# A 192-byte gap per partition moved from in front of H1_hi to in front of HT_hi

## The chip, the cores and the metric

The kernel runs on one core of a Trainium2 chip. The metric is the device time of one execution in microseconds. Five engines work side by side: TensorE (PE in the profile, with its weight loads shown apart as PEld), VectorE (DVE), ScalarE (ACT), GpSimd (POOL) and the queue of SyncE (SP), which issues nearly all transfers.

## The reference

A graph layer over 50,000 nodes of 256 features and 25,000 edges of 64 features, sorted by target node:

```python
h = jnp.maximum(_layernorm(x, axis=-1), 0.0)
agg = segment_sum(edge_attr_64, dst) / maximum(counts, 1)      # mean of a node's edges, 64 wide
combined = concatenate([agg, h], axis=1)                       # 320 wide
hidden = relu(combined @ W1 + b1)                              # 512 wide
out = x + hidden @ W2 + b2                                     # 256 wide
```

## The kernel before, in words

The nodes are worked through in 98 tiles of 512 (the last has 336), two buffers in turn; tiles 2 to 95 run in a hardware loop with two tiles a pass. Each float32 operand is split into a high part that TensorE's float32r format holds and a low part with the rest, and products are taken as high x high + high x low + low x high.

For one tile: VectorE takes the statistics of the rows X (line 673), GpSimd works out scale and shift (437 to 442), ScalarE writes the normalized rows HN (585), four transfers regroup them into HQ, and VectorE turns them to features x nodes, HT (714). ScalarE rounds HT to HT_hi (597), VectorE subtracts to HT_lo (722). The tile's edges arrive by transfers, are scaled and split on GpSimd and ScalarE (E_both), and TensorE sums them per node with a one-hot matrix OH (lines 901 to 906, seven matmuls of 128 columns). ScalarE and VectorE write these edge sums into QA and QB (602, 604, 726, 728).

Layer 1 on TensorE goes over four blocks m of 128 hidden units. Each block takes six matmuls of 512 columns on the nodes (lines 917, 918 and 919, for two halves c) and two on the edge sums (926 and 927). The weights are the stationary operand, which TensorE loads ahead; HT_hi, HT_lo, QA and QB are the moving operand. The edge sums of the next tile stand behind block 1. ScalarE then rounds the rectified block to H1_hi (611) and VectorE writes H1_lo (732). In layer 2 the roles are the other way round: H1_hi and H1_lo are stationary and the weights w2_both are moving, 512 columns (line 940: high and low weights side by side) and then 256 columns (line 942), 16 such pairs per tile. VectorE adds the result to the rows (743, 746), and SyncE stores them.

The order on each engine is the order of the program text; semaphores hold the engines together. SBUF tiles are placed one behind the other in the order in which `sb(...)` is called, each start rounded up to 32 bytes in the partition. From the sizes this gives, for starts modulo 256 bytes: all weights (w1_hi, w1_lo, wa_hi, wb_lo, w2_both) at 64; X, XB, O, HN and HQ at 192; E_both, OH, HT, HT_hi, HT_lo, QA and QB at 128; then the 192 bytes called `beside`, which nothing reads or writes, and H1_hi and H1_lo at 64.

Of the kernel before, what the change touches and what calls it, by code (L numbers as in the profile page):

```python
# [14 lines left out]
P = 128  # L15
# [11 lines left out]
def build(nc, x, src, dst, edge_attr, w1, b1, w2, b2, out):  # L27
# [41 lines left out]
    with ExitStack() as ctx:  # L69
        def sb(name, shape, dt=F32):  # L70
            return ctx.enter_context(nc.sbuf_tensor(name, shape, dt))
# [65 lines left out]
        E_both = [sb(f"E_both{b}", [P, SUB, 2, DE], F32R) for b in range(2)]  # L137
        OH = [sb(f"OH{b}", [P, SUB, P], F32R) for b in range(2)]
        HT = sb("HT", [P, CD, TILE])
        HT_hi = [sb(f"HT_hi{b}", [P, CD, TILE], F32R) for b in range(2)]  # L140
        HT_lo = [sb(f"HT_lo{b}", [P, CD, TILE], F32R) for b in range(2)]
        QA = sb("QA", [P, TILE], F32R)
        QB = sb("QB", [P, TILE], F32R)
        beside = sb("beside", [P, 48])
        H1_hi = sb("H1_hi", [P, CH, TILE], F32R)
        H1_lo = sb("H1_lo", [P, CH, TILE], F32R)

# [50 lines left out]
        def turned(t, c):  # L198

            return P2[c][:] if isinstance(t, int) and t < 2 else HT[:, c, :]  # L200

# [73 lines left out]
        def moved(t, b):  # L275

            if isinstance(t, int):
                return MOVED * (t // 2)
            return MOVED // 2 * t - MOVED // 2 * b
# [387 lines left out]
        def _(dve):  # L667
# [42 lines left out]
            def transpose(t, b, c):  # L710
                if c == 0:
                    past(dve, s_hlo, 2 * t)
                    dve.wait_ge(s_hq[b], moved(t, b))
                dve.transpose(HT[:, c, :].rearrange("p (j n k) -> p k j n", j=SUB, k=QN),  # L714
                              HQ[b][:, :, c * QP:(c + 1) * QP].rearrange("p (k j) f -> p k j f", k=QN)).then_inc(s_th, 1)
# [316 lines left out]
```

## Time and profile before

| | |
|---|---|
| median of 3 runs | 1337.56 us (1337.38 to 1338.96) |
| profiled execution, its own time | 1337.26 us |
| its span, first to last instruction | 1335.7 us |
| mean granted clock of TensorE | 0.997 of full speed |
| busy: PE, PEld, DVE, ACT, POOL | 1319.7, 1118.0, 1216.5, 697.4, 541.7 us |

Busy is the time an engine has an instruction in it; TensorE's matmuls overlap (one starts while the one before still drains), so its busy time says that it never stands still, not that it is at its peak. The distance between the starts of successive matmuls is the better measure of its speed. The profile's line numbers are those of the listing above.

### The profile page before, as it was taken

What the parts mean: (1) busy time and instruction counts of PE and PEld (TensorE: products, weight loads), DVE (VectorE), ACT (ScalarE), POOL (GpSimd) and SP (SyncE); (2) the same over time, 40 slices, a digit from 0 to 9 for tenths busy, and PEclk for the clock granted to TensorE, in tenths of its full rate; (3) what the DMA queues carried; (4) which work ended last, traced back from release to release, by engine and by line L of the source; (5) the groups of instructions that cost most, each with busy time, mean ns of one, the idle gap of its engine ahead of it and who ended that gap; (6) DMA issues with size and microseconds to landing.
All of it is one profiled execution on the core that took longest, in us unless ns stands there. A gap on an engine that the chain in (4) does not pass through costs nothing.

```text
span 1335.7 us, 29289 instructions
## 1 busy us (share of the span) xinstructions
PE 1319.7 (99%) x6998; PEld 1118.0 (84%) x6998; DVE 1216.5 (91%) x3153; ACT 697.4 (52%) x1285; POOL 541.7 (41%) x707
## 2 busy tenths in 40 slices
PE   6999999999999999999999999999999999999998
PEld 4788888888888888888888888888888888888887
DVE  6899999999999999999999999999999999999997
ACT  5455555555555555555555555555555555555553
POOL 6443434343434343434343434343434343434341
PEclk8999999999999999999999999999999999999999
DMA  4676767676767676767676767676767676767663
GB/s 119 126 126 130 126 130 126 130 126 130 125 131 125 131 125 131 125 131 125 131 125 131 124 132 124 132 124 132 124 132 124 132 123 132 123 133 123 133 111 76
DMA packets 420693, 168.21 MB, mean 126 GB/s; under 512 B 319092, under 2 KB 420230, under 8 KB 420680
## 3 DMA queue, kind: packets, MB, share of 16 engines
q1 hardware_dynamic: 419688, 166.89, 67.2%
q10 hardware_dynamic: 992, 1.18, 0.3%
q14 instruction: 9, 0.07, 0.0%
q8 instruction: 4, 0.07, 0.0%
HBM read 66.25 MB, written 51.40 MB: 88 GB/s over the span
## 4 chain that ended last, share of the span: by engine, by line
PE 93%; SPq 3%; DVE 1%; DMA 1%; issue 1%; POOL 0%; ACT 0%; DVEq 0%; POOLq 0%
PE P L940 25%; PE P L942 13%; PE P L917 13%; PE P L919 13%; PE P L918 13%; PE P L926 6%; PE P L927 6%; PE PA L906 1%; PE PA L905 1%; SPq L324 1%; DMA HQ<-HN 1%; SPq L323 1%; SPq L311 1%; SPq L284 0%; PE PA L901 0%
## 5 line engine op out<-in xcount | busy, mean ns | idle before, releaser
L940 PE MATMUL P<-w_both,H_hi 128*128 128x512 f32 x1564 | 548.4, 392 | 2.5 <-DVE H_lo L732 2.4
L611 ACT ACTIVATE H_hi<-P 128x512 fp32r<-128x512 f32 x392 | 233.9, 598 | 490.7 <-PE P L927 490.7
L942 PE MATMUL P<-w_both,H_lo 128*128 128x256 f32 x1564 | 437.8, 280 | 0.0
L940 PEld LDWEIGHTS P<-w_both,H_hi 128*128 128x128 f32 x1564 | 292.5, 187 | 69.5 <-DVE H_lo L732 3.9
L732 DVE SCALAR_TENSOR_TENSOR H_lo<-P,H_hi 128x512 fp32r<-128x512 f32 x392 | 266.0, 679 | 67.7 <-ACT H_hi L611 64.4
L917 PE MATMUL P<-HT_hi,w_hi 128*128 128x512 f32 x776 | 309.0, 398 | 0.0
L918 PE MATMUL P<-HT_lo,w_hi 128*128 128x512 f32 x776 | 303.3, 391 | 0.0
L919 PE MATMUL P<-HT_hi,w_lo 128*128 128x512 f32 x776 | 303.2, 391 | 0.0
L460 POOL TENSOR_TENSOR XB<-X,b_row 128x1024 f32<-128x1024 f32 x97 | 233.9, 2411 | 167.4 <-DVE O L746 166.1
L942 PEld LDWEIGHTS P<-w_both,H_lo 128*128 128x128 f32 x1564 | 295.2, 189 | 3.6
L454 POOL TENSOR_TENSOR E_both<-ES,E_both 128x256 fp32r<-128x256 f32 x98 | 72.5, 740 | 391.7 <-ACT E_both L591 391.7
L714 DVE STREAM_TRANSPOSE HT<-HQ 128x512 f32<-128x512 f32 x192 | 205.2, 1069 | 1.9 <-DMA HQ<-HN 1.8
L585 ACT ACTIVATE HN<-X,shift,rstd 128x256 f32<-128x256 f32 x388 | 200.3, 587 | 4.0 <-POOL shift L442 4.0
L597 ACT ACTIVATE HT_hi<-HT 128x512 fp32r<-128x512 f32 x192 | 121.6, 633 | 118.9 <-DVE HT L714 118.8
L746 DVE TENSOR_TENSOR O<-P,XB 128x256 f32<-128x256 f32 x391 | 166.0, 425 | 13.3
L919 PEld LDWEIGHTS P<-HT_hi,w_lo 128*128 128x128 f32 x776 | 145.7, 188 | 32.5
L917 PEld LDWEIGHTS P<-HT_hi,w_hi 128*128 128x128 f32 x776 | 145.6, 188 | 28.3
L743 DVE TENSOR_TENSOR XB<-P,XB 128x256 f32<-128x256 f32 x391 | 163.4, 418 | 4.6 <-PE P L942 1.5
L918 PEld LDWEIGHTS P<-HT_lo,w_hi 128*128 128x128 f32 x776 | 146.2, 188 | 23.7
L926 PE MATMUL P<-QA,wa_hi 128*128 128x512 f32 x392 | 153.6, 392 | 0.1
L927 PE MATMUL P<-QB,wb_lo 128*128 128x512 f32 x392 | 152.7, 390 | 0.0
L722 DVE TENSOR_TENSOR HT_lo<-HT,HT_hi 128x512 fp32r<-128x512 f32 x192 | 139.0, 725 | 9.1 <-ACT HT_hi L597 0.8
(87 smaller groups left out, 1196.0 us busy)
## 6 DMA issues: line engine op xcount, KB each, us to landing
out_dram<-O SPq DMA_DIRECT2D x97, 512.0 KB, 4.5
HQ<-HN SPq DMA_DIRECT2D x384, 128.0 KB, 4.1
X<-in_x_dram SPq DMA_DIRECT2D x95, 512.0 KB, 4.3
ER<-in_edge_attr_dram SPq DMA_DIRECT2D x392, 32.0 KB, 1.8
DT<-table_dram SPq DMA_DIRECT2D x392, 1.0 KB, 1.7
X<-in_x_dram ACTq DMA_DIRECT2D x1, 512.0 KB, 5.2
w_raw<-in_L_gnn_W_dram ACTq DMA_DIRECT2D x4, 128.0 KB, 5.1
w_raw<-in_L_gnn_W_dram SPq DMA_DIRECT2D x2, 256.0 KB, 4.3
```

The costliest lines, as they stand in the source:

```text
L460: pool.tensor_tensor(XB[b][:], rows_of(t, b), b2_row[:].unsqueeze(1).to_broadcast([P, SUB, D]), ALU.add).then_inc(s_xb, 1)
L585: act.activation(into, rows, ACT.Relu, bias=shift[b][:, j:j + 1], scale=rstd[b][:, j:j + 1]).then_inc(s_ln, 1)
L611: act.activation(H1_hi[:, m, nodes(t)], bank(m)[:, nodes(t)], ACT.Relu).then_inc(s_1hi, 1)
L714: dve.transpose(HT[:, c, :].rearrange("p (j n k) -> p k j n", j=SUB, k=QN), HQ[b][:, :, c * QP:(c + 1) * QP].rearrange("p (k j) f -> p k j ...
L732: dve.scalar_tensor_tensor(out=H1_lo[:, m, nodes(t)], in0=bank(m)[:, nodes(t)], scalar=0.0, in1=H1_hi[:, m, nodes(t)], op0=ALU.max, op1=AL ...
L917: pe.matmul(bank(m)[:, nodes(t)], w1_hi[:, c, cols], HT_hi[b][:, c, nodes(t)], start=(c == 0), stop=False)
L918: pe.matmul(bank(m)[:, nodes(t)], w1_hi[:, c, cols], HT_lo[b][:, c, nodes(t)], start=False, stop=False)
L919: pe.matmul(bank(m)[:, nodes(t)], w1_lo[:, c, cols], HT_hi[b][:, c, nodes(t)], start=False, stop=False)
L926: pe.matmul(bank(m)[:, nodes(t)], wa_hi[:, cols], QA[:, nodes(t)], start=False, stop=False)
L927: pe.matmul(bank(m)[:, nodes(t)], wb_lo[:, cols], QB[:, nodes(t)], start=False, stop=True).then_inc(s_l1, 1)
L940: pe.matmul(out_bank(j)[some, :], H1_hi[:, m, rows], w2_both[:, m, :, :].rearrange("p a d -> p (a d)"), start=(m == 0), stop=False)
L942: last = pe.matmul(out_bank(j)[some, 0:D], H1_lo[:, m, rows], w2_both[:, m, 0, :], start=False, stop=(m == CH - 1))
```

## The change

The allocation of `beside` moves up by four lines of the program. HT_hi, HT_lo, QA and QB then start 192 bytes later, at 64 modulo 256; HT and all before it, and H1_hi and all behind it, keep their addresses. No instruction is added, removed or moved.

```diff
         HT = sb("HT", [P, CD, TILE])
+        beside = sb("beside", [P, 48])
         HT_hi = [sb(f"HT_hi{b}", [P, CD, TILE], F32R) for b in range(2)]
         HT_lo = [sb(f"HT_lo{b}", [P, CD, TILE], F32R) for b in range(2)]
         QA = sb("QA", [P, TILE], F32R)
         QB = sb("QB", [P, TILE], F32R)
-        beside = sb("beside", [P, 48])
         H1_hi = sb("H1_hi", [P, CH, TILE], F32R)
         H1_lo = sb("H1_lo", [P, CH, TILE], F32R)
```

## Rows read from the trace of the kernel before

**Rows 1.** The page: span, busy time of each engine, granted clock in slices, chain by engine.
```profile
span 1335.7 us, 29289 instructions
PE 1319.7 (99%) x6998; PEld 1118.0 (84%) x6998; DVE 1216.5 (91%) x3153; ACT 697.4 (52%) x1285; POOL 541.7 (41%) x707
...
PEclk8999999999999999999999999999999999999999
...
PE 93%; SPq 3%; DVE 1%; DMA 1%; issue 1%; POOL 0%; ACT 0%; DVEq 0%; POOLq 0%
```
**Rows 2.** Groups by line, matmuls: xcount | busy us, mean ns | idle before.
```profile
L940 PE MATMUL P<-w_both,H_hi 128*128 128x512 f32 x1564 | 548.4, 392 | 2.5 <-DVE H_lo L732 2.4
L942 PE MATMUL P<-w_both,H_lo 128*128 128x256 f32 x1564 | 437.8, 280 | 0.0
L917 PE MATMUL P<-HT_hi,w_hi 128*128 128x512 f32 x776 | 309.0, 398 | 0.0
L918 PE MATMUL P<-HT_lo,w_hi 128*128 128x512 f32 x776 | 303.3, 391 | 0.0
L919 PE MATMUL P<-HT_hi,w_lo 128*128 128x512 f32 x776 | 303.2, 391 | 0.0
...
L926 PE MATMUL P<-QA,wa_hi 128*128 128x512 f32 x392 | 153.6, 392 | 0.1
L927 PE MATMUL P<-QB,wb_lo 128*128 128x512 f32 x392 | 152.7, 390 | 0.0
```
**Rows 3.** Busy time per engine in one tile's stretch, with the granted clock.
```profile
core 0: us, PE busy (x) PEld busy (x) DVE busy (x) ACT busy (x) POOL busy (x), PEclk, DMA share, GB/s
661.00:674.36 13.36, 13.36 (x73) 11.37 (x72) 12.35 (x32) 7.06 (x14) 5.39 (x7) 1.00 0.69 128
```
**Rows 4.** Timeline of PE, steady tiles: start us, duration us, what.
```profile
661.18 0.39 PE L918 MATMUL P<-HT_lo,w_hi 128*128 128x512 f32 x1
...
661.63 0.39 PE L926 MATMUL P<-QA,wa_hi 128*128 128x512 f32 x1
...
667.64 0.40 PE L917 MATMUL P<-HT_hi,w_hi 128*128 128x512 f32 x1
...
671.32 0.22 PE L901 MATMUL PA<-OH,E_both 128*128 128x128 f32 x1
...
671.74 0.44 PE L917 MATMUL P<-HT_hi,w_hi 128*128 128x512 f32 x1
672.02 0.39 PE L918 MATMUL P<-HT_lo,w_hi 128*128 128x512 f32 x1
...
675.45 0.39 PE L940 MATMUL P<-w_both,H_hi 128*128 128x512 f32 x1
...
677.53 0.39 PE L940 MATMUL P<-w_both,H_hi 128*128 128x512 f32 x1
...
681.00 0.40 PE L917 MATMUL P<-HT_hi,w_hi 128*128 128x512 f32 x1
...
682.39 0.39 PE L926 MATMUL P<-QA,wa_hi 128*128 128x512 f32 x1
```
**Rows 5.** Timeline of PE, layer 2 of tile 95, behind a wait.
```profile
1306.18 0.50 PE L940 MATMUL P<-w_both,H_hi 128*128 128x512 f32 x1 [0.56 <-DVE H_lo L732]
...
1306.63 0.40 PE L940 MATMUL P<-w_both,H_hi 128*128 128x512 f32 x1
...
1309.82 0.39 PE L917 MATMUL P<-HT_hi,w_hi 128*128 128x512 f32 x1
```
**Rows 6.** Timeline of DVE: last instructions ahead of their readers on PE.
```profile
676.40 0.67 DVE L732 SCALAR_TENSOR_TENSOR H_lo<-P,H_hi 128x512 fp32r<-128x512 f32 x1
...
681.77 0.29 DVE L728 TENSOR_TENSOR QA<-PA,QA 64x128 fp32r<-64x128 f32 x1
```

## The prediction

> **What bounds the kernel now.** I read the page's busy line and its chain of waits first. TensorE (PE) is busy for 99% of the span and holds 93% of the chain that ended last, while VectorE has 91% and ScalarE 52% of the span [rows 1]. The chain changes hands only in the short stretches at the two ends. The groups by line then say what TensorE does: 3,112 matmuls of layer 1, which is 776 on each of lines 917, 918 and 919 and 392 on each of lines 926 and 927, and 2 x 1564 of layer 2 [rows 2]. The reader should not add up their mean durations (about 390 ns each): the matmuls overlap. What counts is the distance from one start to the next, and that is read in the order of time [rows 4]. One tile of 512 nodes takes 681.00 - 667.64 = 13.36 us, and in such a stretch TensorE is covered for 13.36 us of 13.36 with the clock granted in full, VectorE for 12.35 us [rows 3, 4]. So 98 tiles at 13.36 us are 1309 us of the 1335.7, and nothing outside TensorE's own stream moves the end in the steady part.
>
> The steady tile falls into parts, by starts [rows 4]. Layer 1 from 667.64 to 671.32 is 16 matmuls in 3.68 us, the seven edge sums to 671.74 take 0.42 us (60 ns each), the first matmul after them 0.28 us, the next 15 to 675.45 take 3.43 us (228.7 ns each), and layer 2 to 681.00 is 16 pairs (512 and 256 columns) in 5.55 us, which is 346.9 ns a pair. 512 columns at 2.4 GHz are 213.3 ns, so each step of layer 1 carries some 15 ns that are not columns. Only these 15 ns can answer to an address.
>
> **The change, part by part.** It adds and removes no instruction, wait or transfer. The 192 bytes leave the place in front of H1_hi and stand in front of HT_hi. HT_hi, HT_lo, QA and QB move up by 192 bytes, from 128 to 64 modulo 256. H1_hi and everything behind it stay at their addresses, and so do all tiles up to HT. Three things can feel it.
>
> (a) The 3,112 matmuls of layer 1 (and 24 in the prologue) stream their moving operand from another start, while the weights they are paired with stay at 64. This is on the path. The trace of before has no matmul of layer 1 with both operands at 64, so I bound it by neighbours. The floor is the 213.3 ns of the columns: a gain of at most 228.7 - 213.3 = 15.4 ns x 3,112 = 48 us. For the other side there is the most expensive stream in the trace: behind a wait, layer 2 runs from 1306.63 to 1309.82 in 9 pairs, 354.4 ns a pair, against 346.9 [rows 5]. That is 7.5 ns more a pair at the very same addresses, or 3.8 ns a matmul. On 3,112 matmuls of layer 1 it would be a loss of 12 us, and on layer 2's 1564 pairs likewise 12 us; both ends together are -48 and +24 us. The nearest rows for the value itself are layer 2's, because there both operands already start at 64. A straight line through its pairs and the edge sums (60 ns for 128 columns, both operands at 128, so equal start again) is pitch = a + b x columns with a + 128 b = 60 and 2a + 768 b = 346.9. It gives b = 0.443 ns and a = 3.3 ns, and 230.2 ns for 512 columns. Layer 1 shows 228.7 ns with the starts 64 bytes apart. So the rows allow a loss of 1.5 ns per matmul if equal starts are what costs it. The times in the rows are rounded to 10 ns: the edge sums' 0.42 us over 7 steps leave 1.4 ns either way on each, and with it this difference may be zero. I take zero. The two placements that the trace does show agree within what it can resolve, and a tile of one placement has no reason in these rows to be cheaper.
>
> (b) The writers and readers of the moved tiles on ScalarE and VectorE: lines 597, 602 and 604 (ScalarE), 722, 726 and 728 (VectorE). None of them is on the path. The narrowest cover is the edge sums': VectorE's line 728 ends at 681.77 + 0.29 = 682.06 and TensorE wants QA at 682.39, 0.33 us later. The next is layer 2's: H_lo ends at 676.40 + 0.67 = 677.07 and its first reader in that tile, the seventh pair, starts at 677.53, 0.46 us later [rows 4, 6]. Their time would have to grow by over 0.3 us a tile before TensorE waits; four VectorE instructions stand in that sum (two of line 722, one each of 726 and 728), so each would have to take some 80 ns longer. If it came to that, each further 0.1 us a tile is 9.8 us. I cost it at nothing.
>
> (c) DMA: the row tiles X, HN, HQ and O, the edge windows and the output don't move. No transfer writes or reads a moved tile. Nothing.
>
> The sum is 0 us on the profiled execution's own 1337.26 us (span 1335.7 and 1.6 us around it), which is 0.3 us under the median of 1337.56. I forecast 1337.5 us.
>
> Against an effect of (a) speaks the Trainium skill, SBUF — State Buffer, section "Who interferes with whom": TensorE has two independent read ports, one for the moving operand and one for weight loads, and waits for nobody. By that rule the distance between the two starts cannot matter and the sum stays 0. What the rows add: at one and the same set of addresses a pair costs 346.9 or 354.4 ns [rows 4, 5], so something other than the address sets part of the step; that is consistent with the rule but doesn't prove it.
>
> **The rivals.** *Equal starts cost a little.* Mechanism and place: layer 1 falls onto the line of layer 2 and the edge sums, 230.2 in place of 228.7 ns. Price: 1.5 ns x 3,112 = 4.7 us, or 1342 us; it decides as soon as the step exceeds 229.6 ns (0.9 ns is 2.7 us). For it: two streams with equal starts lie on one line and layer 1 lies under it. Against: the rounding above, and no view names the cause. *Layer 1 hands over in another rhythm, and layer 2 falls into its dear one.* The rows show that layer 2 keeps 354.4 ns a pair from the wait to the end of its stage, so the rhythm holds once entered. The steady tile has 346.9 now. Entered in every tile it costs 7.5 ns x 1564 = 11.7 us: 1349 us. This case and the one before are the other side of the forecast.
>
> *Layer 1 gets cheaper.* Its steps aren't even now: from 661.18 to 661.63 are two steps of 225 ns, where the mean is 228.7 [rows 4]. If the new placement lets all of them run so, it is 3.7 ns x 3,112 = 11.5 us: 1326 us. For it: the short steps exist, and the columns alone would allow more. Against: layer 2, already with equal starts at 64, has no shorter steps than layer 1. *The extra goes altogether.* The step could fall to the columns' own 213.3 ns and a few more; at half of the 15.4 ns the gain is 24 us, 1314 us. Of it the Trainium skill says, TensorE: Matmul & The Clock Gate, section "Back-to-back issue gap", that the warm distance is N / 2.4 + 2.5 ns, 215.8 ns for 512 columns; by that the kernel's layer 1 has 12.9 ns to give, 40 us on 3,112 matmuls, as an estimate from that page. The trace doesn't agree with the figure in any 512-column step, with weights and rows at 64 or at 128, so I give it little. *The change doesn't do what it says:* the order of the tiles sets their addresses, and 128 + 192 is 64 modulo 256; this ends at no change too, and I leave it 2%.
>
> **How the numbers follow.** About 0.2%, 2.7 us, is what a measurement of this kernel can tell from no change. No change 42% (with the 2%), equal starts cost a little 18%, the dear rhythm in layer 2 or in layer 1 14%, shorter steps 22% (from a third of the 11.5 us up), the extra goes altogether 4%. That makes faster 0.26, same 0.42, slower 0.32. The range reaches from 1327 to 1347 us: it holds no change, the 4.7 us and most sizes of both partial cases, and leaves out the full dear rhythm, the full 11.5 us of gain and the large gain. Inside "no change" alone it would be 1336 to 1340 us.
>
> **What the changed profile would show.** If I am right: 13.36 us from one tile's first layer 1 start to the next, 3.43 us for the 15 steps behind the edge sums, 5.55 us for the 16 pairs, no wait before line 926 or 940 in steady tiles, and counts as before. The first rival shows 3.45 us and 13.41 us a tile, with layer 2 as it is. The second shows 5.67 us for the 16 pairs. The third shows under 3.40 us. Line 722's or 726's mean longer by more than 80 ns, with TensorE waiting at line 926, would say that the cover of (b) was the weak step. I am wrong if the tile differs from 13.36 us by more than 0.028 us.

## The result and the profile after

The changed kernel takes 1342.59 us (median of 7 runs, 1341.61 to 1343.77) against 1337.56 for the kernel before (7 runs): ratio 1.0036, 95% interval 1.0026 to 1.0045. The profiled execution took 1342.59 us with a span of 1341.0, against 1337.26 and 1335.7. It is slower by some 5 us, where no change was forecast.

The page's busy time, chain and clock of the changed kernel answer to [rows 1] and say what they said there: TensorE is the bound, with a mean granted clock of 0.998 of full speed and the same instructions.

```profile
span 1341.0 us, 29289 instructions
PE 1324.8 (99%) x6998; PEld 1118.4 (83%) x6998; DVE 1217.3 (91%) x3153; ACT 697.0 (52%) x1285; POOL 541.4 (40%) x707
...
PEclk9999999999999999999999999999999999999999
...
PE 93%; SPq 3%; DVE 1%; DMA 1%; issue 1%; POOL 0%; ACT 0%; DVEq 0%; POOLq 0%
```

Where in the run the time went is read from two starts of the same matmul far apart, the first matmul of tile 4 and the first of tile 95. In the timeline of the kernel before:

```profile
79.80 0.40 PE L917 MATMUL P<-HT_hi,w_hi 128*128 128x512 f32 x1
...
1295.56 0.40 PE L917 MATMUL P<-HT_hi,w_hi 128*128 128x512 f32 x1
```

and of the changed one:

```profile
80.45 0.40 PE L917 MATMUL P<-HT_hi,w_hi 128*128 128x512 f32 x1
...
1301.06 0.40 PE L917 MATMUL P<-HT_hi,w_hi 128*128 128x512 f32 x1
```

Over these 91 tiles it is 1220.61 - 1215.76 = 4.85 us, 53 ns a tile; 0.65 us was lost ahead of them and 0.2 us won back behind. So it is a loss of the steady tile. The groups by line of the changed kernel, the answer to [rows 2], point at layer 2 but not at its size, since mean durations of overlapping matmuls say little:

```profile
L940 PE MATMUL P<-w_both,H_hi 128*128 128x512 f32 x1564 | 557.1, 398 | 3.1 <-DVE H_lo L732 2.9
L942 PE MATMUL P<-w_both,H_lo 128*128 128x256 f32 x1564 | 438.9, 281 | 0.0
L917 PE MATMUL P<-HT_hi,w_hi 128*128 128x512 f32 x776 | 308.5, 398 | 0.0
L918 PE MATMUL P<-HT_lo,w_hi 128*128 128x512 f32 x776 | 303.6, 391 | 0.0
...
L926 PE MATMUL P<-QA,wa_hi 128*128 128x512 f32 x392 | 152.5, 389 | 0.1
```

The timeline of the changed kernel's TensorE shows it; it answers to [rows 4], start first:

```profile
670.64 0.40 PE L917 MATMUL P<-HT_hi,w_hi 128*128 128x512 f32 x1
...
674.29 0.22 PE L901 MATMUL PA<-OH,E_both 128*128 128x128 f32 x1
...
674.70 0.45 PE L917 MATMUL P<-HT_hi,w_hi 128*128 128x512 f32 x1
674.99 0.40 PE L918 MATMUL P<-HT_lo,w_hi 128*128 128x512 f32 x1
...
678.41 0.39 PE L940 MATMUL P<-w_both,H_hi 128*128 128x512 f32 x1
...
678.75 0.40 PE L940 MATMUL P<-w_both,H_hi 128*128 128x512 f32 x1
...
683.70 0.40 PE L940 MATMUL P<-w_both,H_hi 128*128 128x512 f32 x1
...
684.05 0.40 PE L917 MATMUL P<-HT_hi,w_hi 128*128 128x512 f32 x1
```

Layer 1's first half is 3.65 us (before 3.68), its 15 steps from 674.99 are 3.42 us (3.43), and layer 2 is 5.64 us (5.55). From the starts in whole nanoseconds, in nearly every steady tile, layer 1 with the edge sums went from 7.809 to 7.773 us and layer 2 from 5.551 to 5.640. Layer 1, whose operand was moved, became 36 ns cheaper. Layer 2, none of whose addresses changed, became 89 ns dearer: 14 pairs in 683.70 - 678.75 = 4.95 us are 353.6 ns each, close to the 354.4 ns that [rows 5] gave behind a wait. 89 - 36 is the 53 ns.

### The profile page after: what moved, and what is told of

Read it like the earlier page. It is cut to its first block, busy times and chain, and to the rows that moved or that the text cites. A ratio compares the mean times of both kernels' runs of the same rounds, so it can differ in the third digit from the quotient of the medians.

```text
span 1341.0 us, 29289 instructions
## 1 busy us (share of the span) xinstructions
PE 1324.8 (99%) x6998; PEld 1118.4 (83%) x6998; DVE 1217.3 (91%) x3153; ACT 697.0 (52%) x1285; POOL 541.4 (40%) x707
## 4 chain that ended last, share of the span: by engine, by line
PE 93%; SPq 3%; DVE 1%; DMA 1%; issue 1%; POOL 0%; ACT 0%; DVEq 0%; POOLq 0%
PE P L940 26%; PE P L942 13%; PE P L917 13%; PE P L918 13%; PE P L919 13%; PE P L926 6%; PE P L927 6%; PE PA L906 1%; PE PA L905 1%; SPq L323 1%; DMA HQ<-HN 1%; SPq L324 1%; SPq L311 1%; SPq L284 0%; PE PA L901 0%
## 5 line engine op out<-in xcount | busy, mean ns | idle before, releaser
L940 PE MATMUL P<-w_both,H_hi 128*128 128x512 f32 x1564 | 557.1, 398 | 3.1 <-DVE H_lo L732 2.9
L714 DVE STREAM_TRANSPOSE HT<-HQ 128x512 f32<-128x512 f32 x192 | 210.3, 1095 | 1.7 <-DMA HQ<-HN 1.6
L722 DVE TENSOR_TENSOR HT_lo<-HT,HT_hi 128x512 fp32r<-128x512 f32 x192 | 136.0, 709 | 12.1 <-ACT HT_hi L597 7.7
```

Source lines behind the costliest of these rows:

```text
L940: pe.matmul(out_bank(j)[some, :], H1_hi[:, m, rows], w2_both[:, m, :, :].rearrange("p a d -> p (a d)"), start=(m == 0), stop=False)
```

## The experiments

Theory A: the step depends on how weight loads and row stream of TensorE run against each other, through the starts modulo 256 of both and through the timing with which a stage is entered. Theory B: another engine's traffic on the moved tiles disturbs TensorE. "Rows" are the moving operand and "weights" the stationary one; "difference" below is the start of the rows minus the start of the weights, modulo 256. A stream is "settled" when its steps repeat in a fixed pattern.

**Streams by themselves.** A new kernel; its core:

```python
for so in range(0, 64, 16):            # start of the weights, in floats
    for mo in range(0, 64, 16):        # start of the rows
        same(so, mo, 512, 24)          # 24 matmuls of 512 columns
        mark()                         # one small matmul as a mark
# then pairs(so, mo, 12) in the same way; pairs(16, 16, 12) behind mark(64), mark(96), ...
```

> A kernel of its own that leaves the whole computation out: one TensorE runs matmul streams over constant data while all other engines stand still. 24 steps of 512 columns for each pair of starts (weights, rows) at 0, 64, 128 and 192 modulo 256; then 12 pairs of 512 and 256 columns for each of the 16; then such pairs at 64/64 behind one shorter matmul of 64 to 336 columns; then streams of 128, 256 and 384 columns, and one in bf16. Theory A (timing between weight loads and rows inside TensorE, set by both starts): steps at 64 (weights) and 128 (rows) take 228.7 ns as layer 1 did before, steps at 64/64 take 226.7 ns as after, and pairs at 64/64 take 346.9 or 352.5 ns depending on the matmul that they follow. Theory B (the other engines' reads and writes of SBUF slow TensorE down): all 16 placements agree, near 216 ns a step and 325 ns a pair. If starts matter by themselves and not by history, the pairs behind the shorter matmuls all take the same time.

It took 261.17 us. Its timeline on TensorE, for weights at 64 and rows at 0, 64, 128 and 192 in this order (line 67 is the mark):

```profile
38.59 5.83 PE L56 MATMUL A<-R,W 128*128 128x512 f32 x24
44.26 0.19 PE L67 MATMUL A<-R,W 128*64 128x64 f32 x1
44.29 5.71 PE L56 MATMUL A<-R,W 128*128 128x512 f32 x24
49.84 0.19 PE L67 MATMUL A<-R,W 128*64 128x64 f32 x1
49.87 5.76 PE L56 MATMUL A<-R,W 128*128 128x512 f32 x24
55.47 0.19 PE L67 MATMUL A<-R,W 128*64 128x64 f32 x1
55.49 5.82 PE L56 MATMUL A<-R,W 128*128 128x512 f32 x24
61.15 0.19 PE L67 MATMUL A<-R,W 128*64 128x64 f32 x1
```

From the first start to the mark it is 5.67, 5.55, 5.60 and 5.66 us. All 16 placements fall into four groups by the difference alone: 0 gives 5.55 to 5.57 us, 64 gives 5.59 to 5.60, 128 gives 5.65 to 5.66, 192 gives 5.67 to 5.68. Settled, that is 226.7, 228.8, 232.7 and 233.3 ns a step (means over the last 12 steps, from starts in whole nanoseconds). Layer 1 stood at difference 64 before and at 0 after. Settled streams at starts 64 and 64 with fewer columns took 120.0 ns (256 columns) and 173.3 ns (384), by the starts in whole nanoseconds. A bf16 stream comes last in this kernel:

```profile
252.08 5.35 PE L73 MATMUL A<-RB,WB 128*128 128x512 bf16 x24
257.08 0.38 PE L67 MATMUL A<-R,W 128*64 128x64 f32 x1
```

From the first of its 24 starts to the last it is 4.974 us, 216 ns a step. That is the figure which the Trainium skill gives for the warm gap of an isolated matmul (TensorE: Matmul & The Clock Gate, section "Back-to-back issue gap"). The same section has some 131 ns a matmul of 512 columns for a sustained stream with weight loads; no run here shows that, and the streams measured here lie at the isolated figure (bf16) or some 11 to 17 ns above it (float32r).

The pairs at 64/64, behind six matmuls of 512 columns and a mark of 64 columns, and behind the same with a mark of 96:

```profile
177.60 0.39 PE L61 MATMUL A<-R,W 128*128 128x512 f32 x1
...
181.07 0.39 PE L61 MATMUL A<-R,W 128*128 128x512 f32 x1
...
183.36 0.39 PE L61 MATMUL A<-R,W 128*128 128x512 f32 x1
...
186.89 0.40 PE L61 MATMUL A<-R,W 128*128 128x512 f32 x1
```

Ten pairs take 3.47 us in one (first two lines) and 3.53 us in the other, at the same addresses in the same kernel, and each keeps its pace to the end. Marks of 64, 128, 160, 192 and 256 columns led to some 347 ns a pair, 96, 224 and 336 to some 353. So with equal starts there are two rhythms, and the entry picks. The cheap one, 346.7 ns, is the sum of two settled steps, 226.7 and 120.0 ns; the dear one, 353.3, has some 6.6 ns more in every pair. Theory B falls for the stream's pace: nothing else ran here.

**The model tile.** TensorE alone runs the steady tile's matmuls:

```python
tiles(ht=32, qa=32, qb=32)   # starts in floats: the kernel before
tiles()                      # all at 16 floats = 64 bytes: the changed kernel
tiles(ht=32)                 # edge sums only
tiles(qa=32, qb=32)          # rows only
```

> A kernel of its own that leaves the computation out: TensorE alone runs the matmuls of the steady tile in the kernel's order (two layers, edge sums), three tiles per variant, over constant data, with nothing to wait for. Theory A (everything is inside TensorE and follows from the starts and the order): the first four variants, with the starts of the kernel before, of the changed kernel, of edge sums only and of rows only, take 13.36, 13.41, 13.41 and 13.49 us a tile. If another engine's traffic has a part in it, they differ from these. Further variants look for a cheaper tile with rows, edge sums, layer 1 results and weights all at 64: layer 2's long and short matmuls grouped or in alternating order, edge sums behind another block, QB alone or H1_lo alone at 0, 128 or 192, and H1_hi, H1_lo and w2_both together at 0, 128 or 192. By theory A layer 1 keeps 7.77 us in most and layer 2 takes either 5.55 or 5.64 us. Last come steps of 512 columns with 128, 64 and 32 columns of weights: if the extra over 216 ns comes from weight loads that read beside the rows, it shrinks with their width; if it is a property of the row stream, it stays.

It took 895.26 us. The last tile of each of the first two variants, from its first matmul (line 68) to the mark (line 53):

```profile
45.01 0.40 PE L68 MATMUL A<-HT_hi,w_hi 128*128 128x512 f32 x1
...
58.38 0.19 PE L53 MATMUL A<-w_hi 128*64 128x64 f32 x1
...
85.32 0.40 PE L68 MATMUL A<-HT_hi,w_hi 128*128 128x512 f32 x1
...
98.73 0.19 PE L53 MATMUL A<-w_hi 128*64 128x64 f32 x1
```

In nanoseconds the four tiles are 13,361, 13,413, 13,415 and 13,486; the kernels' own are 13,360, 13,413, 13,413 and 13,487. The 53 ns come back to a nanosecond or two with every other engine idle. The model's tiles lie at other places of SBUF than the kernel's and agree with them modulo 256, so that is enough. The same kernel varied the width of the weights: with 128 columns the 24 steps took 5.55, 5.60, 5.66 and 5.67 us at the four differences, with 64 or 32 columns 5.53 to 5.57 us at all of them. The spread between the starts shrinks from 0.13 to 0.04 us and no longer follows the difference; the extra over bf16 stays. The first fits a collision with weight loads, which no run shows by itself; the second says that most of the extra doesn't come with their width.

**Parts of the change, other starts.** The edits are gaps only (48 floats are 192 bytes):

```diff
 e2   gap [P, 48] before QA; none elsewhere              (QA, QB 64; HT_hi, HT_lo 128)
 e3   gap [P, 48] before HT_hi, [P, 16] before QA, [P, 48] before H1_hi   (the reverse)
 e6   gap [P, 32] before HT_hi, [P, 16] before H1_hi     (rows and edge sums 0)
 e7   no gap                                             (H1_hi, H1_lo 128)
 e8   the changed kernel, and [P, 48] before H1_lo       (H1_lo 0)
```

> Only QA and QB begin at 64; HT_hi and HT_lo stay at 128, H1_hi at 64. Theory A: layer 2's rhythm is set by how layer 1 hands over, and the last two matmuls ahead of it read QA and QB. If these two alone set it, layer 2 takes 5.64 us a tile and layer 1 stays near its 7.81 us: 1345 to 1346 us. If the rhythm of the whole layer 1 sets it, layer 2 keeps 5.55 us, some 1337 us. Theory B (the addresses that ScalarE and VectorE write beside layer 2): as HT_hi and HT_lo are three quarters of what they write there, at most a quarter of the 5 us: 1338 to 1339 us.

> HT_hi and HT_lo begin at 64, QA and QB at 128, H1_hi at 64. Theory A with the last two matmuls as the deciding ones: layer 2 keeps 5.55 us and layer 1 takes between 7.77 and 7.81 us, 1334 to 1337.5 us. With the whole of layer 1 as the deciding one: layer 2 5.64 us, 1342 to 1344 us. Theory B: three quarters of the loss, 1341 to 1342 us.

> HT_hi, HT_lo, QA and QB begin at 0 modulo 256, H1_hi and the weights at 64 as before. Theory A by the stream measurements (rows minus weights of 192: 233.2 ns a step against 228.9 at 64 and 226.6 at 0): layer 1 takes 32 x 4.3 = 0.14 us a tile more than in the kernel before, 7.94 to 7.96 us, which is 1351 us, or 1360 us if layer 2 also falls into its dear rhythm. Theory B (the address alone that the other engines write, with no relation to the weights): no reason for a longer layer 1, 1337 to 1343 us.

> No gap at all: HT_hi to QB stay at 128 as in the kernel before, H1_hi and H1_lo begin at 128 too, so layer 2 has rows (w2_both at 64) minus weights of 192. Theory A by the stream measurements: 353.3 ns a pair in place of 346.9, 16 x 6.4 = 0.10 us a tile, 1347 to 1348 us, with layer 1's stage unchanged. If layer 2's rhythm depends only on how layer 1 hands over, nothing changes: 1337.5 us.

> The changed kernel, with a second gap of 192 bytes in front of H1_lo, which then begins at 0 modulo 256; HT_hi, HT_lo, QA, QB, H1_hi and the weights at 64. The model tile of this placement took 13.340 us (layer 1 7.79, layer 2 5.55) against 13.413 for the changed kernel's. Theory A: the kernel's steady tile does the same to some ns, 1337.3 - 96 x 0.020 = 1335.4 us, so the loss is undone without touching what the change moved. Theory B: H1_lo's start has nothing to do with the tiles that the change moved, 1342.6 us stays.

The parts are distances between starts in whole nanoseconds, of the commonest tile of each kernel, in us. Each ratio is taken against runs of the kernel before made beside it, whose medians were 1337.56 us for the changed kernel, e2 and e3, 1337.04 for e6 and e7, and 1337.62 for e8:

| kernel | layer 1 | layer 2 | tile | median us | ratio, 95% interval |
|---|---|---|---|---|---|
| before | 7.809 | 5.551 | 13.360 | 1337.56 | |
| changed | 7.773 | 5.640 | 13.413 | 1342.59 | 1.0036 (1.0026 to 1.0045) |
| e2 edge sums only | 7.857 | 5.556 | 13.413 | 1341.78 | 1.0035 (1.0023 to 1.0046) |
| e3 rows only | 7.845 | 5.642 | 13.487 | 1348.59 | 1.0090 (1.0072 to 1.0108) |
| e6 rows, edge sums at 0 | 7.915 | 5.558 | 13.473 | 1348.80 | 1.0087 (1.0069 to 1.0105) |
| e7 no gap | 7.798 | 5.648 | 13.446 | 1345.15 | 1.0059 (1.0041 to 1.0077) |
| e8 H1_lo at 0 | 7.757 | 5.596 | 13.353 | 1336.97 | 0.9996 (0.9986 to 1.0005) |

e2 is a miss of both forms of theory A as I had written them: the edge sums alone cost the same 53 ns a tile, but in layer 1, not in layer 2. There rows and edge sums differ in start, so each block switches the difference twice, and the steps around a switch are long (231 to 237 ns in place of 225 to 232). e3 pays both and is a miss too: 1348.59 us, where the dearest case that I had written was 1344. Layer 2 is dear in e3 and cheap in e2, so it follows the rows' start and not that of the last two matmuls ahead of it. The model tile, run after these two, gives both, so it is theory A without a shortcut. e6 and e7 are doses: difference 192 costs 0.106 us in layer 1 (0.14 forecast; not every step is a settled one, which would explain the rest) and 0.097 us in layer 2 (0.10 forecast). Both kernels came out 2 to 3 us under their forecasts of 1351 and 1347 to 1348 us. e8 undoes the loss by moving a tile that the change never touched; my expectation there quotes the neighbouring variant (H1_lo at 128, 13.340), while the model tile of H1_lo at 0 was 13.353 to 13.354, and the kernel gives 13.353.

**The hand-over by itself.** One extra matmul between the layers of the changed kernel, with 128 columns of weights and of rows (e4) or 64 of each (e12, shown here):

```diff
+                if not (isinstance(t, int) and t < 2):
+                    pe.matmul(PS[0:64, 0, 0:64], wa_hi[:, 0:64], w1_hi[:, 0, 0:64], start=True, stop=True)
                 layer2(t)
```

> The changed kernel with one more matmul of 128 columns (into a PSUM tile that nothing reads then) between layer 1 and layer 2 of each tile from the third on. It costs about 60 ns a tile, 5.8 us. Theory A: the hand-over is another one, so layer 2's rhythm may leave the dear one; if it does, 5.55 us instead of 5.64 us, and the kernel takes 1340 us, less than the changed kernel in spite of the extra work; if not, 1348 us. Theory B: layer 2 keeps 5.64 us, 1348 us.

> The changed kernel with one more small matmul (64 columns of weights, 64 of rows) between layer 1 and layer 2, into a PSUM tile that nothing reads then. Behind just such a matmul layer 2's pairs ran at 346.7 ns in one stream and at 353 in others with equal starts. It costs some 40 to 60 ns a tile. If the hand-over picks layer 2's rhythm and this one picks the cheap one, layer 2 drops from 5.64 to 5.55 us and the kernel takes about 1339 us, less than the changed kernel with more work; if it keeps the dear one, 1347 us.

e4 took 1352.87 us (ratio 1.0115, 1.0097 to 1.0133), above both cases of its expectation. Its pairs stay dear, 353.6 ns: the entry was moved, but not to one of those that lead to the cheap rhythm. And the extra matmul cost 120 ns a tile, not 60: it has 57 ns to itself, and the first pair behind it takes 402 ns in place of 340. e12 took 1344.49 us (1.0053, 1.0038 to 1.0069), between the 1339 and 1347 us of its two cases; the layer 2 of one of its tiles:

```profile
665.70 0.19 PE L960 MATMUL PS<-w_hi,wa_hi 128*64 128x64 f32 x1
665.73 0.48 PE L940 MATMUL P<-w_both,H_hi 128*128 128x512 f32 x1
666.04 0.28 PE L942 MATMUL P<-w_both,H_lo 128*128 128x256 f32 x1
666.16 0.40 PE L940 MATMUL P<-w_both,H_hi 128*128 128x512 f32 x1
...
671.01 0.40 PE L940 MATMUL P<-w_both,H_hi 128*128 128x512 f32 x1
```

14 pairs in 4.85 us are 346.4 ns against the changed kernel's 353.6, at the same addresses. The first pair is paid for with 0.43 us in place of 0.34, so the kernel doesn't gain, but the rhythm is flipped by the hand-over alone, with layer 1 as it was (7.773 us).

**Cheaper tiles.** First the order inside a hidden block (long, short, short, long; e9), whose edit is shown cut to its core, then another search with the model tile (e10), which differs from the first in its list of variants:

```diff
-                        pe.matmul(out_bank(j)[some, :], H1_hi[:, m, rows], ...)       # 512 columns
-                        last = pe.matmul(out_bank(j)[some, 0:D], H1_lo[:, m, rows], ...)  # 256
+                        for high in ((True, False) if m % 2 == 0 else (False, True)):
+                            ...
```

> The changed kernel with layer 2's two matmuls of a hidden block in alternating order: long, short, short, long, and so on, the same work at the same addresses. The model tile took 13.316 to 13.320 us (7.75 and 5.57). Theory A: 1337.3 - 96 x 0.042 = 1333.3 us, faster than both kernels. Theory B: the order inside layer 2 changes nothing, 1342.6 us. A third outcome: TensorE now waits for H1_lo in the first pass, some 0.1 us a tile, 1343 us.

> The model tiles again, TensorE alone, the computation left out: 24 variants, to find the cheapest. All in alternating order first: H1_lo alone, H1_hi with H1_lo and w2_both, or QB at 0, 128 and 192; the starts of the kernel before; edge sums behind another block; one-hot matrix and edge rows at equal and unequal starts. By theory A each gives a tile between 13.25 and 13.50 us, and the plain alternating order repeats 13.316 to 13.320 us. If the figures are not repeatable, it does not.

e9 took 1335.03 us (0.9980, 0.9971 to 0.9990), 1.7 us over the forecast; half its tiles are the model's 13.320, the other half 13.347. e10 (947.62 us) repeated the alternating tile at 13.317 to 13.320, and its cheapest variant was in the kernel's own order, 13.296 to 13.300. The dearest model tile of both searches was 13.527, with QB alone at 0. e11 is the cheapest variant in the kernel: H1_hi and w2_both at 192, H1_lo at 128, the rest as the changed kernel.

```diff
+        gap_w2 = sb("gap_w2", [P, 32])
         w2_both = sb("w2_both", [P, CH, 2, D], F32R)
+        gap_after = sb("gap_after", [P, 32])
...
+        gap_ht = sb("gap_ht", [P, 48])
         HT_hi = ...
-        beside = sb("beside", [P, 48])
+        gap_h1 = sb("gap_h1", [P, 32])
         H1_hi = ...
+        gap_h1lo = sb("gap_h1lo", [P, 48])
         H1_lo = ...
```

> The changed kernel's order, untouched; only starts differ: rows and edge sums (HT_hi, HT_lo, QA, QB) and layer 1's weights at 64, H1_hi and w2_both at 192, H1_lo at 128 modulo 256. It was the cheapest of the model tiles: 13.296 to 13.300 us (layer 1 7.752, layer 2 5.544 to 5.548). Theory A: the kernel's tile takes 13.30 us, 1337.3 - 96 x 0.062 = 1331.4 us, faster than the kernel before and than every version so far. Theory B (other engines' traffic): no relation to the model, 1337 to 1348 us.

It took 1333.41 us: ratio 0.9970 (against 1337.09 us), interval 0.9959 to 0.9982, the lowest median of all and faster than both kernels. Layer 2 is the model's 5.548 us. Layer 1 is 7.752 in some tiles and 7.785 in most, so 2 of the 6 us that were forecast are missing. The long steps lie around the first use of QA, and the cover there had shrunk. VectorE's last write of QA and the weight load that waits for it, first in the changed kernel:

```profile
671.38 0.29 DVE L728 TENSOR_TENSOR QA<-PA,QA 64x128 fp32r<-64x128 f32 x1
671.80 0.19 PEld L926 LDWEIGHTS P<-QA,wa_hi 128*128 128x128 f32 x1
```

then in e11, whose lines are four further on:

```profile
640.83 0.29 DVE L732 TENSOR_TENSOR QA<-PA,QA 64x128 fp32r<-64x128 f32 x1
641.17 0.19 PEld L930 LDWEIGHTS P<-QA,wa_hi 128*128 128x128 f32 x1
```

The load starts 130 ns behind VectorE's end there and 50 ns here. In e9 the two kinds of tile part by this distance: in all 44 tiles of 13.347 us it is 52 or 53 ns and the load starts 1.145 us behind the tile's first matmul, in all 48 of 13.320 us it is 54 to 59 ns and the load starts after 1.140 or 1.141 us. In e11 it is 52 or 53 ns in all 56 tiles with a layer 1 of 7.785 us, but in some of the 21 cheap ones too. The other nine kernels have 62 ns or more in every steady tile, and 52 or 53 ns only for the loads of tiles 3 and 96, for which the list of waits names VectorE's line 728: it is the distance of a load that was held up. So a load held up by 4 ns for VectorE, with the settled steps broken behind it, fits e9 tile by tile and e11 in part; no run moved VectorE's end by itself, so the cause isn't shown.

## Why the prediction was wrong, point by point

- **Bound and place.** Right: TensorE's own stream in the steady tile, no new wait, (b) and (c) at nothing. The 0.33 us of cover in (b) was read from the wrong event, though: the wait sits on the weight load, which starts a step earlier, so the cover was 682.16 - 682.06 = 0.10 us (and layer 2's 0.46 us were 0.35, by the load at 677.42). The load in the timeline of the kernel before, and its entry in that kernel's list of waits (us in total, times, longest):

```profile
682.16 0.19 PEld L926 LDWEIGHTS P<-QA,wa_hi 128*128 128x128 f32 x1
...
PEld P L926 <- DVE QA L728: 0.5, 2, 0.3
```

- **The step that failed is (a), "I take zero".** It asked what one step costs at the new start and read layer 2 and the edge sums as neighbours. Two things in it were wrong. Equal starts don't cost 230.2 ns but 226.7, less than the 228.7 of before. The straight line went wrong at its lower end: the edge sums have, but for the first, 64 columns of weights and take 60 ns, while 128 columns of rows with 128 columns of weights take 112 ns (end of this document), so they don't lie on one line with the pairs. Layer 2's pairs of before, 346.9 ns, do fit settled steps at equal starts, 226.7 + 120.0. And a stage's cost is not a price per step. "Only these 15 ns can answer to an address" looked at layer 1 alone, and layer 2 changed by 89 ns without any change of its own. The tile moved by 0.053 us, beyond the 0.028 that I had named as the sign of being wrong.
- **First rival.** Its total, 1342 us, is what was measured, and its mechanism is refuted: layer 1 became cheaper, by 36 ns a tile. The right total is luck.
- **Second rival.** This is what happened to layer 2: 353.6 ns a pair in every steady tile, 5.64 us against the 5.67 that I had named. It was priced at 11.7 us; 89 ns x 94 tiles are 8.4 us, and layer 1's gain of 36 ns x 94 = 3.4 us pays part back. I had the row that showed two rhythms at one set of addresses and used it as a bound only.
- **Third rival.** Its mechanism holds for layer 1, whose settled steps fell from 228.8 to 226.7 ns, but at a third of its size, 3.4 of 11.5 us; that layer 2 would answer it had not in view.
- **The extra goes altogether.** It didn't: the settled steps stay at 226.7 ns. The 215.8 ns that the prediction took from the Trainium skill are given there for an isolated matmul, which the prediction left out.
- **The rule on ports.** The Trainium skill (SBUF — State Buffer, "Who interferes with whom") has two independent read ports on TensorE. By the streams the pace does depend on the distance between the starts of the two operands, by up to 6.6 ns of 227, so the measurement decides against reading that rule as "no relation". That TensorE isn't disturbed by other engines' traffic agrees with the model tile, which gives the kernel's tile to 2 ns with the others idle.
- **Range and chances.** 1342.6 us lies in the range of 1327 to 1347, but only because a loss of 8.4 us and a gain of 3.4 us that the sum didn't have partly cancel. The side was wrong: no change had 0.42, slower 0.32.

**Open.** Why float32r steps carry some 10 ns more than bf16's 216 at the best start, which part of TensorE holds the rhythm, and what exactly in the entry picks it.

## What to carry to other kernels

Where TensorE never waits, measure starts against starts, stage by stage: the mean duration of overlapping matmuls doesn't give the size of a loss of 1.6%, which is layer 2's here. Moving a tile by some bytes can change a stage that doesn't read it, because a stage's pace hangs on how it is entered; so "nearest row" prices hold only for the same history. A model that runs TensorE's matmuls alone, in order and with the right starts, gave the steady tiles of five kernels to 2 ns, and tried some forty variants in under two milliseconds of device time. In two more kernels, e9 and e11, part of the tiles were 27 and 33 ns longer than the model's: what other engines do to the order of time it can't see.

## What the runs showed of the hardware

- float32r matmuls of 512 columns with 128 columns of weights: 226.7, 228.8, 232.7 and 233.3 ns a step for rows minus weights of 0, 64, 128 and 192 bytes modulo 256, the same for each of the four starts of the weights; bf16, at one placement, 216 ns.
- Pairs of 512 and 256 columns at equal starts have two lasting rhythms, 347 and 353 ns; which one depends on the matmuls ahead of them.
- With 128 columns in the rows as well as in the weights, 24 steps take 2.71 us (112 ns each when settled), nearly twice the 60 ns of the kernel's edge sums with 64 columns of weights. The timeline of the streams kernel:

```profile
222.13 2.88 PE L56 MATMUL A<-R,W 128*128 128x128 f32 x24
224.84 0.20 PE L67 MATMUL A<-R,W 128*64 128x64 f32 x1
```
